# A fused state-space and quantised-FFN kernel: the output stage is moved into the next window, both transposes into the second product, and four staging buffers are cut or widened

## The reference

```python
u = LN(x) @ W_in.T; h1 = silu(LN(x) @ W_sel_in.T)          # 256, 512 wide
a, b, c, d = split(h1 @ W_sel_out.T)                        # 4 x 256
h[t] = sigmoid(a)[t] * h[t-1] + tanh(b)[t] * u[t]           # scan over tokens
x2 = x + LN((tanh(c) * h + d_param * sigmoid(d) * u) @ W_out.T)
q  = LN(x2), then round to 127 levels per token             # act_quant
g  = silu(depthwise_conv3(q @ ternary(w1).T))               # 4096 wide
out = x2 + LN(act_quant(g) @ ternary(w2).T)                 # act_quant again per token
```

## Time and profile before

| what | us |
|---|---|
| median of 3 runs (3447.0 to 3454.6) | 3448.2 |
| the profiled execution | 3456.1 |
| its span, slowest core (the others 3428 to 3446) | 3454.6 |
| PE, DVE, ACT, POOL busy | 1629, 1575, 1232, 552 |

### The profile page before, as it was taken

How to read it: one execution, slowest core, us unless ns; L and a number is a source line. 1 busy time by engine, 2 the same in 40 slices (tenths; PEclk the granted TensorE clock), 3 DMA queues, 4 the chain that set the end, 5 groups by cost and what they waited for, 6 DMA issues and landing times.

```text
span 3454.6 us, 35519 instructions; the slowest of 8 cores (3428.2 to 3454.6 us)
## 1 busy us (share of the span) xinstructions
PE 1629.3 (47%) x8414; PEld 869.6 (25%) x8464; DVE 1575.1 (46%) x4636; ACT 1231.6 (36%) x1961; POOL 552.3 (16%) x849
## 2 busy tenths in 40 slices
PE   0000014465656564646555655555556565655553
PEld 0000013141414141414141423232323232323130
DVE  1130225645454545454545463636363636364462
ACT  1333334433343433333434343434342424232121
POOL 0000001202020202020202020202020202020102
PEclk9999996576767787867676777676867676767775
DMA  5555620212121213121212121212121212121213
GB/s 172 176 171 175 201 79 19 74 42 82 41 81 42 83 40 86 37 83 40 80 43 78 45 77 46 73 49 71 52 73 50 69 53 55 56 55 55 74 37 98
DMA packets 112700, 260.34 MB, mean 75 GB/s; under 512 B 12656, under 2 KB 12656, under 8 KB 112496
## 3 DMA queue, kind: packets, MB, share of 16 engines
q1 hardware_dynamic: 97808, 212.97, 21.2%
q0 software_dynamic: 10080, 36.70, 3.8%
q10 hardware_dynamic: 4608, 8.39, 0.6%
HBM read 232.85 MB, written 25.17 MB: 75 GB/s over the span
## 4 chain that ended last, share of the span: by engine, by line
DMA 23%; PE 20%; DVE 20%; DVEq 10%; ACT 10%; issue 9%; POOL 3%; ACTq 2%; POOLq 2%; SPq 0%
DMA w2sb<-w2s 13%; DVEq L57 10%; PE pE L798 6%; PE pD L990 5%; PE pE L990 4%; DMA stgF<-w1T 4%; DVE h L834 4%; DVE h L842 3%; DVE h L826 3%; DVE accP L861 2%; DMA stgF<-w2T 2%; DMA w2s<-stgb 2%; ACTq L57 2%; POOL h L974 2%; POOLq L57 2%
## 5 line engine op out<-in xcount | busy, mean ns | idle before, releaser
L990 PE MATMUL pD<-w2sb,h 128*128 128x512 bf16 x1006 | 424.3, 514 | 499.6 <-DMA w2sb<-w2s 353.4
L798 PE MATMUL pE<-xqw,w1t 128*128 128x258 bf16 x4352 | 575.5, 297 | 95.2 <-ACT hpre L807 91.4
L798 PEld LDWEIGHTS pE<-xqw,w1t 128*128 128x128 bf16 x4352 | 459.9, 107 | 204.4 <-issue 107.0
L990 PE MATMUL pE<-w2sb,h 128*128 128x512 bf16 x1008 | 444.5, 535 | 43.8 <-DMA w2sb<-w2s 27.7
L807 ACT ACTIVATE hpre<-pE 128x258 bf16<-128x258 f32 x544 | 190.4, 386 | 511.7 <-DVE h L842 358.1
L974 POOL TENSOR_SCALAR h<-k2i,onec,rccn 128x512 bf16<-128x512 int32 x272 | 264.5, 972 | 607.1 <-ACT k2i L970 562.8
L754 DVE COPY xqw<-xqw 128x8 bf16<-128x8 bf16 x16 | 3.0, 185 | 701.8 <-ACT xqw L747 701.8
L970 ACT ACTIVATE k2i<-k2f,rcc 128x512 int32<-128x512 bf16 x272 | 196.2, 722 | 287.7 <-DVE k2f L959 180.7
L990 PEld LDWEIGHTS pD<-w2sb,h 128*128 128x128 bf16 x1024 | 72.8, 103 | 848.5 <-issue 848.1
L959 DVE TENSOR_TENSOR k2f<-h,bc 128x256 bf16<-128x256 bf16 x544 | 235.9, 473 | 62.3 <-ACT k2i L970 51.7
L826 DVE TENSOR_SCALAR h<-hpre,cwt,cbt 128x256 bf16<-128x256 bf16 x544 | 155.8, 350 | 213.1 <-ACT hpre L807 197.2
(11 more groups left out here) (177 smaller groups left out, 2099.4 us busy)
## 6 DMA issues: line engine op xcount, KB each, us to landing
w2sb<-w2s SPq DMA_DIRECT2D x544, 256.0 KB, 2.7
xin<-x SPq DMA_DIRECT2D x16, 1024.0 KB, 5.0
stgF<-w1T POOLq DMA_DIRECT2D x32, 512.0 KB, 4.1
stgF<-w1T SPq DMA_DIRECT2D x32, 512.0 KB, 4.4
stgF<-w2T POOLq DMA_DIRECT2D x32, 512.0 KB, 4.3
stgF<-w2T SPq DMA_DIRECT2D x32, 512.0 KB, 4.5
out<-stgF SPq DMA_DIRECT2D x32, 512.0 KB, 2.9
w2s<-stgb ACTq DMA_DIRECT2D x16, 256.0 KB, 4.5
```

Source lines behind the costliest of these rows:

```text
L798: lambda e, S, c=c, k=k, off=off, pf=pf: e.matmul(pE[:, off:off + 258], w1t[:, 4096 * k + 128 * c:4096 * k + 128 * (c + 1)], xqv[:, pf, k, :],
L990: coff=coff: e.matmul(bank[:, 512 * jj:512 * (jj + 1)], h4[:, 256 * c + 128 * s:256 * c + 128 * (s + 1)], w2sb[:, coff:coff + 512], start= ...
```

## The change

Seven edits. (1) `stgb` is 2048 wide, one half for each s, and GpSimd's wait for the first transpose before it fills the second half is gone. (2) `k2f` is gone: the token scale is multiplied into h4 in place, without VectorE's waits for ScalarE. (3) All 16 pairs are emitted ahead of the second product. (4) `accP` and `accN` are 256 wide: one chunk is folded at a time, eight chunks late instead of four, so that eight chunks are left for the tail. `accF` and `s2row` are replaced by `accP` and a piece of `tad`. (5) In the seventh step of `attn_gen`, sum and square sum of x2 go to the end of the sixth step, ahead of the window's pairs; the layer norm of the next tile goes behind the scale chain, and so does the load of x for tile i + 2. (6) The second product yields after chunks 11 and 23 instead of after 11 and at its end, so that the transposes stand between chunks 23 and 24. (7) Of the output stage, what follows the eviction is a function `emit_z8b`, which the next window calls first.

```diff
-        stgb = sb("stgb", [128, 1024], BF16)
+        stgb = sb("stgb", [128, 2048], BF16)
-        k2f = sb("k2f", [128, 2 * 512], BF16)
-        accP = sb("accP", [128, 512], BF16)
-        accN = sb("accN", [128, 512], BF16)
-        accF = sb("accF", [128, 256], BF16)
-        s2row = sb("s2row", [1, 256], F32)
+        accP = sb("accP", [128, 256], BF16)
+        accN = sb("accN", [128, 256], BF16)
...
-            issue_x_dma(i + 2, wait_gp=P_x2[i][1], wait_ac=A_xin1[i])
-            yield
-
-            q.drain("v")
-            for s in range(NSUB):
-                q.op("v", lambda e, S, s=s, i=i: e.reduce_max(
...
             a_sum3 = q.cnt["ac"]
-            emit_ln1_prep(i + 1)
+            yield
+
             q.wait("v", "ac", a_sum3)
+            q.drain("v")
+            for s in range(NSUB):
+                q.op("v", lambda e, S, s=s, i=i: e.reduce_max(
...
+            emit_ln1_prep(i + 1)
+            issue_x_dma(i + 2, wait_gp=P_x2[i][1], wait_ac=A_xin1[i])
             yield
...
             for s in range(NSUB):
-                if s == 1:
-                    q.wait("g", "pe", PE_T2[i][0])
...
+            emit_z8b(f - 1)
...
-                    if c >= 7:
-                        cp = c - 4
+                    if c >= 11:
+                        cp = c - 8
...
-                        for hh in (0, 512):
-                            gsl = h4[:, 256 * (cp - 3) + hh:256 * (cp - 3) + hh + 512]
+                        for hh in range(4):
+                            gsl = h4[:, 256 * (cp - 3 + hh):256 * (cp - 2 + hh)]
...
-            for hh in (0, 512):
-                gsl = h4[:, 256 * 28 + hh:256 * 28 + hh + 512]
+            for cc in range(24, 32):
+                gsl = h4[:, 256 * cc:256 * (cc + 1)]
...
-            def emit_pair(p2):
+            for p2 in range(16):
...
-                if p2 >= 2:
-                    q.wait("v", "ac", A_anc[f][p2 - 2])
-                elif f > 0:
-                    q.wait("v", "ac", A_anc[f - 1][14 + p2])
-                q.drain("v")
...
-                    vtt = q.op("v", lambda e, S, cc=cc, fsl=fsl: e.tensor_tensor(
-                        fsl, h4[:, 256 * cc:256 * (cc + 1)], bc2[:, :], OP.mult),
+                    hsl4 = h4[:, 256 * cc:256 * (cc + 1)]
+                    vtt = q.op("v", lambda e, S, hsl4=hsl4: e.tensor_tensor(
+                        hsl4, hsl4, bc2[:, :], OP.mult),
...
-            for p2 in range(6):
-                emit_pair(p2)
             for c in range(32):
-                if c >= 12 and c % 2 == 0:
-                    emit_pair(c // 2)
...
-                if c == 11:
+                if c == 11 or c == 23:
                     yield
             PE_w2[f] = PE_w2c[f][31]
-            yield
...
             q.drain("a")
+
+        def emit_z8b(f):
...
             q.wait("a", "dv", P_x2[min(f + 1, ntr - 1)][0])
             for s in subs:
-                src = stgF[:, 1024 * s:1024 * (s + 1)]
...
             for _ in win_gen(ntr):
                 pass
+            emit_z8b(ntr)
```

More of the change, by code:

```diff
@@ L310, in weight_pass @@
                 else:
-                    dstb = stgb[:, :] if p % 2 == 0 else selh[:, 0:1024]
+                    dstb = stgb[:, 0:1024] if p % 2 == 0 else selh[:, 0:1024]
                     if p >= 2:
@@ L724, in attn_gen @@
                     q.drain("g")
-                    q.op("g", lambda e, S, h=h: e.tensor_scalar(
-                        stgb[:, 512 * h:512 * (h + 1)], stgi[:, :],
+                    bsl = stgb[:, 1024 * s + 512 * h:1024 * s + 512 * (h + 1)]
+                    q.op("g", lambda e, S, bsl=bsl: e.tensor_scalar(
+                        bsl, stgi[:, :],
                         onec[:, 0:1], rccn[:, 0:1], OP.mult, OP.add))
                     q.drain("g")
-                    P_uq1[i][hi] = q.op("g", lambda e, S, s=s, h=h: e.tensor_scalar(
-                        stgb[:, 512 * h:512 * (h + 1)], stgb[:, 512 * h:512 * (h + 1)],
+                    P_uq1[i][hi] = q.op("g", lambda e, S, s=s, bsl=bsl: e.tensor_scalar(
+                        bsl, bsl,
                         sc("G1", s), zeroc[:, 0:1], OP.mult, OP.add), sem="gp")
@@ L734, in attn_gen @@
                 for cc in range(8):
-                    PE_T2[i][s] = q.op("t", lambda e, S, cc=cc: e.matmul(
+                    PE_T2[i][s] = q.op("t", lambda e, S, s=s, cc=cc: e.matmul(
                         pC[:, 128 * cc:128 * (cc + 1)],
-                        stgb[:, 128 * cc:128 * (cc + 1)],
+                        stgb[:, 1024 * s + 128 * cc:1024 * s + 128 * (cc + 1)],
                         identb[:, :], start=True, stop=True),
@@ L1015, in win_gen @@
             q.drain("a")
+        def emit_z8b(f):
+            if f < 0:
+                return
+            have_a = f > 0
+            have_b = f < ntr
+            subs = ([0] if have_a else []) + ([1] if have_b else [])
             q.wait("a", "dv", P_x2[min(f + 1, ntr - 1)][0])
             for s in subs:
-                src = stgF[:, 1024 * s:1024 * (s + 1)]
-                q.op("a", lambda e, S, s=s, src=src: e.activation(
-                    stgA[:, :], src, AF.Square, accum_out=sc("SSQF", s)), sem="ac")
+                src_ = stgF[:, 1024 * s:1024 * (s + 1)]
+                q.op("a", lambda e, S, s=s, src_=src_: e.activation(
+                    stgA[:, :], src_, AF.Square, accum_out=sc("SSQF", s)), sem="ac")
                 q.drain("a")
@@ L1023, in win_gen @@
             q.wait("v", "ac", a_sqf)
-            g_chF = stat_chain("v", "F", subs[0], len(subs), var_scale_col="G2")
-            q.wait("a", "dv", g_chF)
+            V_chF[f] = stat_chain("v", "F", subs[0], len(subs), var_scale_col="G2")
+            q.wait("a", "dv", V_chF[f])
             a_apF = 0
```

38 lines of the change are left out of this document (16 added, 22 removed).

## The result

The changed kernel takes 3638.9 us (median of 10 runs, 3635.3 to 3674.9) against 3448.0 before (10 runs): a ratio of 1.057, 95% interval 1.054 to 1.059. It is slower by 191 us. The forecast was slower by 85, 3534 us, with a range of 3490 to 3580. The direction was right and the size was not. The profiled execution has a span of 3638.1 us, core 6, with a granted clock of 0.756 to 0.771 over the cores, as before (0.756 to 0.770).

A forecast was written before the change was run, and what follows sets the result against it. It took a serial chain, VectorE in the first product and w2 loads in the second as bounds. 104 + 39 - 37 + 121 - 158 + 13 + 3 = +85 on 3448.2 gave about 3534 us, range 3490 to 3580.

The forecast's parts named there:

- What bounds the kernel: One iteration, 174.2 us: a serial chain, a first product owned by VectorE, a second product waiting for w2 loads.
- Narrow folds: First product and tail: four 256-wide fold pairs replace two 512-wide ones per group; +104 us, bounds 60 and 147.
- Transposes' block and end of the product: Whole block now interrupts the second product between chunks 23 and 24, +121 us; the product's end gets shorter, -158.
- the rival had 84: Transposes' block hidden, ScalarE making the second half's integers during TensorE's matmuls: 84 us less, 3450; chance 0.06.
- The output stage deferred: Start of the next window, stage behind the next tile's transposes: 9.2 us against 9.9, -0.7 an iteration.
- Sums ahead of the pairs: Start of second product: ScalarE's sums and squares delay the first pair by 2.6 us, 15 times, +39.
- Pairs early: Second product: GpSimd takes 1.23 us a pair beside VectorE's multiplications, one is used each 4.31 us, so hidden.
- the rival was on the page with 8 us a window: GpSimd kept out by the lock until VectorE's 32 multiplications end: 8 us, 17 times, 3670; chance 0.04.
- Rows 5: Profile rows before the change: four convolution instructions take 2.85 us beside GpSimd's additions, against 1.12; cited against the lock rule.
- The load of x: Second product: load moves from ahead of w2's load 2 to load 14, 1.0 us, 13 times, +13 (0 to 33).
- Early pairs, the wait at chunk 12: Second product: TensorE's wait for a GpSimd pair at chunk 12 goes, the w2 load is late next; -37 us.
- once: Tile 0: the layer norm of tile 1 ends behind the scale chain and ScalarE quantises behind it, some +3 us.

The follow-up runs named there:

- e4: Changed kernel with the folds 512 wide and one group of four chunks behind, as before the change: 3541.4 us.
- e8: As e7, with a third place for w2's chunks and load 2 issued ahead of the pairs: 3102.9 us.
- e10: Changed kernel with the transposes' block back behind chunk 31, as before the change: 3666.4 us.
- e2: Changed kernel with all four quantisations on ScalarE and GpSimd ahead of the transposes and their evictions: 3533.8 us.
- e6: Changed kernel with the second half of the output stage back at the end of its own window: 3641.1 us.
- e12: Changed kernel with both the paced multiplications of e1 and the sums behind the sixth pair of e3: 3527.1 us.
- e1: Changed kernel with VectorE's multiplications, from the third pair on, again waiting for ScalarE's copy two pairs before: 3552.5 us.
- e11: Changed kernel with a single wait in VectorE's row of 32 multiplications, the fifth waiting for ScalarE's copy of the first pair: 3551.4 us.
- e3: Changed kernel with ScalarE's four sums put back behind the sixth pair, the multiplications still one unbroken row: 3526.8 us.
- e9: Changed kernel with the load of x issued right behind the second addition to x2, as before the change: 3600.2 us.
- e7: Changed kernel with e1, e2, e3, e4 and e9 joined: 3286.7 us, ratio 0.953 to the kernel before.
- e5: Changed kernel with 30 probe rows of 32 VectorE instructions behind its last tile, GpSimd additions released at varied moments; its whole time says nothing.

## Why the forecast was too low, point by point

- **What bounds the kernel: right.** VectorE owns the first product (e4), the loads of w2 the second (e8), and the serial chain counts in full at its end (e10).
- **Narrow folds: right.** +104 forecast, 98 measured (e4).
- **Transposes' block and end of the product: right.** That the whole block stays because ScalarE's queue, and not `stgb`, holds it was the step on which the sign hung; e2 shows that it is so and what the other order would give (105, the rival had 84). +121 and -148 together are -27, and e10 gives 27, with both terms in its rows.
- **The output stage deferred: mis-sized**, -10 forecast; the -2 measured (e6) can't be told from nothing.
- **Sums ahead of the pairs: mis-sized by themselves**, 39 forecast and 25 measured (e12). And they have a second effect that the forecast did not have, in the next point.
- **Pairs early: the failed step.** The forecast wrote that GpSimd "takes 1.23 us for a pair beside VectorE's multiplications; the product uses up one each 4.31 us, so that is hidden". That row is of the kernel before, in which VectorE stopped for ScalarE every second pair and GpSimd asked amid its first few multiplications. The change took those stops away (edit 2) and at the same time moved GpSimd's request from 1.9 us into the row to 4.2 (edit 5). Each alone is harmless: with the breaks back the late request costs no more than its sums (e1, e11), with the early request back the unbroken row costs nothing (e3). Together they keep GpSimd out to the end of the row: 86 us. The row of windows 15 and 16 could not be seen ahead of time, but the rival was on the page with 8 us a window. The Trainium skill (SBUF — State Buffer, on the shared port pair) says that the side that issues second is blocked until the first one's instruction ends. By that rule GpSimd would get in after one multiplication of 0.42 us; here it was out for the nineteen that were left, and where it did get in it was 0.66 us late (1.43 against 0.77). The measurement decides: when GpSimd asks late in an unbroken row of multiplications, it does not get in between two of them. Rows 5, which stood beside the rule in the forecast, are another case: VectorE's tensor_scalar with one input tensor, beside GpSimd's fp32 additions with two.
- **The load of x: mis-sized.** 13 us forecast, 39 measured (e9), a little beyond the bound of 33; part of it falls in chunks ahead of the load and is not explained. I had priced it by the difference of two places at which it collides; at its old place in the changed kernel it collides with nothing, and in e7, where the product starts earlier, chunks 0 to 12 take 26.6 us against e9's 26.0, so hardly anything there either.
- **Early pairs, the wait at chunk 12: right.** -37 forecast. It was not undone by itself, but the traces have it: chunks 0 to 12 of core 6 take 28.8 us before and 26.0 in e9, where the load of x stands in its old place; 2.8 us less in each of 13 windows, 36, window 0 not counted.
- **Sum.** With the measured sizes: 98 + 25 + 86 - 27 - 2 + 39 + 3 (once, not measured) - 36 = 186, against 191; five us are less than six comparisons can tell. Of the miss of 106 us, 86 are the lock and 26 the load of x; the others come to -6.

## What to carry to other kernels

Before taking a wait off an engine that can keep another one out, look at what moment of its row the other one asks for its turn: a duration read in a row with pauses says nothing of one without. Here one wait behind the fourth multiplication was enough, and the waits cost nothing (e12, which has them, is level with e3, which has not). And when a buffer is doubled, check that the queues are written in an order that uses it: in this kernel one loop split was worth 105 us.

## What the runs showed of the hardware that I had not expected

- GpSimd's access beside a row of two-input VectorE instructions depends on when it asks: by the sixth multiplication (1.94 us) it took turns, one addition of 1.43 us to three multiplications; from the seventh (2.27 us) it was out to the row's end, 9.19 us at most. At 2.09 us both happened, one in and seven out of eight cores, and one of 128 requests at 1.76 to 1.82 us was kept out (e3).
- Once in, it stays in: nine additions in a row, to the end of 28 multiplications (e11).
- VectorE's one-input tensor_scalar (bf16) delays it by 0.05 to 0.2 us only, whenever it asks (e5). The other way round, four of them took 2.85 us instead of 1.12 beside GpSimd's two-input fp32 additions (at 2234.00).
- With up to three loads of w2 out on each of eight cores instead of two, a load of 256 KB took 3.0 us instead of 2.7, and the second product's chunks came every 1.4 to 1.5 us instead of 2.2 (e8, e7).
